# A fused Flamingo block: two PSUM banks for E slots in all stages, four for score units with 512 keys

## The reference, cut to what matters

```python
x = x + tanh(g_xattn[0]) * cross_attention(layernorm(x), ctx)      # att0: 512 keys
x = x + tanh(g_ffn[0])   * moe_top1(layernorm(x))                  # m0: 8 experts, hidden 512, ReLU
# a decoder layer on h = layernorm(x), added to x with tanh(g_xattn[1]):
h = ln(h + self_attention(h))                                      # att1: 256 keys
h = ln(h + cross_attention(h, ctx))                                # att2: 512 keys
h = ln(h + relu(h @ fc1 + b1) @ fc2 + b2)                          # f: hidden 512
# a second block on x, its output added to x with tanh(g_ffn[1]):
x = x + causal_rope_attention(rmsnorm(x))                          # att3: 256 keys
x = x + moe_top2(rmsnorm(x))                                       # m1: 4 experts, hidden 384, SiLU-gated
# each attention: softmax(q @ k.T / sqrt(8)) @ v, over all keys, head by head
```

## Time and profile before

| | before |
|---|---|
| median of 3 runs | 1185.59 us (1184.12 to 1190.38) |
| the profiled execution | 1189.5 us |
| its span, first to last instruction | 1187.5 us |
| granted TensorE clock, mean | 0.95 |
| busy: TensorE / VectorE / ScalarE / GpSimd | 1049.7 / 790.0 / 621.8 / 367.8 us |
| score matmuls, 512 keys (L1637) | 512, 403 ns each |
| maxima, 512 keys (L1304) | 512, 685 ns each |
| E matmuls (L1672) | 1408, 284 ns each |
| exponentials (L1110) | 768, 578 ns each |

### The profile page before, as it was taken

The page is one execution under the profiler, slowest core; times in us unless marked ns, Lnnn a source line. Parts: engine busy times, 40 slices in busy tenths (PEclk is TensorE's granted clock), DMA queues, the critical chain, the costliest instruction groups (busy, mean ns, idle before and its releaser), DMA issues. The chain is left out here.

```text
span 1187.5 us, 25293 instructions
## 1 busy us (share of the span) xinstructions
PE 1049.7 (88%) x8548; PEld 645.7 (54%) x8548; DVE 790.0 (67%) x1935; ACT 621.8 (52%) x1331; POOL 367.8 (31%) x982
## 2 busy tenths in 40 slices
PE   4999998799898698788799998897988889899998
PEld 1455554477454486445455554444555667656665
DVE  4788887533877524577688877869666777644443
ACT  1477764455564454456477775655644445543221
POOL 4333332221434422543433333413233435200000
PEclk9999998899987799788899999999998999999999
DMA  6655644464334663565665563543435355301000
GB/s 164 190 161 174 178 144 137 127 180 135 107 104 125 198 181 111 157 175 157 205 182 176 155 175 95 167 123 104 125 94 152 114 165 155 109 28 46 11 26 9
DMA packets 173173, 157.97 MB, mean 133 GB/s; under 512 B 13075, under 2 KB 146835, under 8 KB 172691
## 3 DMA queue, kind: packets, MB, share of 16 engines
q1 hardware_dynamic: 168854, 141.24, 40.4%
q0 software_dynamic: 4192, 15.12, 4.1%
HBM read 91.56 MB, written 66.85 MB: 133 GB/s over the span
## 5 line engine op out<-in xcount | busy, mean ns | idle before, releaser
L1110 ACT ACTIVATE prob<-ps 128x512 f32<-128x512 f32 (+1 forms) x768 | 400.2, 578 | 177.1 <-PE ps L1672 134.4
L1304 DVE TENSOR_REDUCE nmax<-ps 128x1 f32<-128x512 f32 x512 | 328.9, 685 | 82.6 <-PE ps L1637 81.3
L1672 PE MATMUL ps<-Qst,Kst 75*128 75x256 bf16 x1408 | 244.8, 284 | 15.8 <-DMA Qst<-mrow 8.7
L1637 PE MATMUL ps<-Kst,Qst 72*128 72x512 bf16 x512 | 198.7, 403 | 24.2 <-DVE nmax L1304 21.3
L1688 PE MATMUL av_ps<-prob,Vx 128*32 128x256 f32 (+1 forms) x3072 | 215.8, 398 | 0.6 <-ACT FB L1187 0.3
L1672 PEld LDWEIGHTS ps<-Qst,Kst 75*128 75x128 bf16 x1408 | 135.7, 101 | 86.5 <-ACT prob L1110 15.5
L1688 PEld LDWEIGHTS av_ps<-prob,Vx 128*32 128x32 f32 x3072 | 91.8, 114 | 66.4 <-issue 33.9
L1034 POOL TENSOR_TENSOR mparts<-nmax,zeros 128x8 bf16<-128x8 f32 x122 | 25.2, 206 | 306.1 <-issue 298.6
L1313 DVE TENSOR_REDUCE nmax<-ps 128x2 f32<-128x512 f32 x128 | 85.6, 687 | 47.9 <-PE ps L1651 47.2
L1637 PEld LDWEIGHTS ps<-Kst,Qst 72*128 72x128 bf16 x512 | 50.5, 99 | 106.6 <-DVE nmax L1304 53.2
L1114 ACT ACTIVATE OT<-av_ps 128x256 f32<-128x256 f32 x128 | 49.2, 385 | 108.7 <-PE av_ps L1688 108.1
(11 more groups left out here) (198 smaller groups left out, 1652.9 us busy)
## 6 DMA issues: line engine op xcount, KB each, us to landing
q_parts<-qp SPq DMA_DIRECT2D x96, 192.0 KB, 2.5
Qst<-q_parts SPq DMA_DIRECT2D x128, 144.0 KB
k_parts<-kp SPq DMA_DIRECT2D x46, 384.0 KB, 3.3
Kst<-k_parts SPq DMA_DIRECT2D x60, 288.0 KB
k_parts<-kp SPq DMA_DIRECT2D x48, 192.0 KB, 2.7
Kst<-k_parts SPq DMA_DIRECT2D x64, 144.0 KB
ctxT<-in_ctxT SPq DMA_DIRECT2D x16, 256.0 KB, 4.8
xs_rows<-in_blank SPq DMA_DIRECT2D x22, 128.0 KB, 4.1
```

Source lines behind the costliest of these rows:

```text
L1110: act.activation(prob[:, RING_AT[st] % RING, half * 512:half * 512 + w], bank(x)[:, 0:w], ACT.Exp).then_inc(drained(x), 1)
L1304: ve.tensor_reduce(nmax[:, g, u, h % GH:h % GH + 1], bank(st), AX.X, ALU.max, negate=True).then_inc(drained(st), 1)
L1637: last = pe.matmul(bank(st), Qst[0:ROWS, par, s, u * P:u * P + P], Ks[0:ROWS, par, s, :], start=True, stop=True)
L1672: last = pe.matmul(o, Ks[0:KROWS, par, h, t * P:t * P + P], Qst[0:KROWS, par, h, :], start=True, stop=not a.rope)
```

## The change

E steps are allowed banks 0 and 1 in every stage. Score units are allowed banks 2 to 5 with 512 keys (four in place of three), and 2 to 4 with 256 keys, as before. The smaller steps, m0.h, f.h and m1.h keep their sets, so bank 2 is now shared between score units and m0.h and f.h in stages with 512 keys too.

```diff
-    at, uses, last, low, split = {}, [0] * BANKS, list(range(-BANKS, 0)), 3, 6
+    at, uses, last, split = {}, [0] * BANKS, list(range(-BANKS, 0)), 6
     for i, st in enumerate(STEPS):
         if st[0] == "S":
-            low, split = (3, 6) if att(st[1]).keys == SC else (2, 5)
+            split = 6 if att(st[1]).keys == SC else 5
         if st[0] in E_KINDS:
-            takers, allowed = ((st, 0), (st, 1)), range(5 if st[0] == "m1.h" else low if st[0] == "E" else 3)
+            takers, allowed = ((st, 0), (st, 1)), range(5 if st[0] == "m1.h" else 2 if st[0] == "E" else 3)
         elif st[0] == "S":
-            takers, allowed = (st,), range(low, split)
+            takers, allowed = (st,), range(2, split)
```

## The result

| | before | after |
|---|---|---|
| median (range) of 5 runs | 1185.59 us (1182.02 to 1191.73) | 1209.18 us (1193.31 to 1214.32) |
| ratio to before, 95% interval | | 1.0145 [1.0097, 1.0194] |
| the profiled execution | 1189.5 us | 1209.6 us |
| its span | 1187.5 us | 1207.8 us |
| granted TensorE clock, mean | 0.95 | 0.935 |

A forecast was written before the change was run, and what follows sets the result against it. TensorE was taken to set the pace with VectorE close behind; 25.3 us of E-step costs less 20.4 us of score-unit gains made it 4.9 us slower, 1190.5 us against the 1185.6 median, range 1180 to 1201.

The forecast's parts named there:

- the direct sum: Whole kernel: 25.3 us of E-step costs minus 20.4 us of score-unit gains, so 4.9 us slower.
- the dismissal of the clock: Rival, 600 to 843 us: new pauses bring three stretches at 1.2 GHz, 10 us worse than the sum, 1200.5; chance 0.06.
- a clock below 1.00 between 600 and 843 us: Sign in the third attention stage's windows that the forecast is wrong and the clock rival holds.
- The stretch of 655 to 684 us: One batch: right if 0.5 to 1 us longer; if not, costs are covered; over 1.5 us, scores wait again.
- Cost of E's two banks: E steps on all stages wait longer for exponentials, with 1.1 us for the hidden-layer step: 25.3 us in all.
- The pair: Two E steps with only two score units between: second half's load 0.49 us later, 29 pairs, 14.2 us.
- The slots of 1.31 us: E steps with four transposes also between them: second half waits 0.19 us more in 23 slots, 4.4 us.
- Gain of the fourth score bank: Score units' 53.2 us of waits for maxima on VectorE, less those that stay: 20.4 us gained.
- "score waits" rival: Units arrive in bunches at VectorE; only 8 of the 20 us gained, 17 us slower, 1202.5; chance 0.13.
- The bank that the dense block's hidden layer shares with scores: At 771.74 us the hidden-layer step waits for a maximum to leave its bank: 1.1 us, once.
- 736 to 756 and 811 to 831 us: VectorE nearly full, score waits 9.0 and 8.6 us: 1.8 us gained each, 14.0 of 17.6 stay.
- 178 to 202 us: Behind the routing plan on VectorE, 7.1 us in five score waits: 3.8 gained, 3.3 lost.

The follow-up runs named there:

- before_look2: The kernel before, unedited, in a second further profile to see how bodies vary with nothing changed: one execution of 1201.93 us.
- e9: The changed kernel with the score units of body 16 alone back on three banks: 1.0134 against the kernel before, median 1204.99 us.
- e3: The kernel before with E steps on two banks in all stages and scores left on three: 1.0114 against the kernel before, median 1200.56 us.
- after again: The changed kernel, unedited, run once more beside the kernel before: ratio 1.0149, median 1218.98 us.
- e2: The kernel before with the change made in the third attention stage (att2) alone: 1.0068 against the kernel before, median 1196.29 us.
- e1: The kernel before with the change made in the first attention stage (att0) alone: 1.0108 against the kernel before, median 1196.73 us.
- e8: The kernel before with the dense block's activations moved from the exponentials' ring to an idle buffer: 0.9949 against before, 1194.35 us; repeated, 0.9971, 1184.57 us.
- e5: The kernel before with a fourth score bank at 512 keys, bank 6, shared with the smaller steps: 1.0983 against the kernel before, median 1318.78 us.
- e4: The kernel before with scores on four banks and E left on three, sharing bank 2: 1.0102 against the kernel before, median 1201.92 us.

## Why the prediction was wrong, point by point

**The sign was the likeliest one, the size was not.** Two steps failed. One is in the direct sum: the waits that a fourth score bank takes away were counted as time, 20.4 us of gain where the runs show 0.6, and with the cost of E's banks put too high as well the sum is some 12 us where 4.9 was forecast, as the paragraphs below work out. The other is the dismissal of the clock: "Against it: from 736 to 756 us TensorE is busy only 15.2 of 20 us, with waits for VectorE through the whole window, and the clock stays full". That row shows that waits of one kind at one place are harmless, not that new ones elsewhere will be. And the trace before has some 120 us at 1.2 GHz outside att2, so that it "does not agree for this kernel" was too much to say. I gave this rival 0.06, and in the bodies that can be compared it holds 6 of 17 us in one profile and 9 of 21 in the other: 2 to 4 us in body 4 and 3 to 5 in att2 (277.5 and 279.6 against 274.2, which is before plus the 9.2 worked out below). The forecast's own test, a clock below 1.00 between 600 and 843 us, names it. But `before_look2` has such a clock with nothing changed, so this sign alone would not have shown it. The stretch of 655 to 684 us, body 18, is 1.0 us longer, as the forecast said.

The Trainium skill's rule, "TensorE: Matmul & The Clock Gate", section "A second HAM failure mode: psum-queue depth-cycling", was cited and set aside. After, the trace agrees with it as far as the clock goes (0.51 in 606 to 613 us), and in e9 the number of banks in rotation decides how long that stretch is. That short pauses between groups of matmuls bring it about no run here shows: the pause ahead of it is one of 1.47 us, for a DMA.

**Cost of E's two banks, 25.3 us: too high by more than half.** The pair itself is right: 0.88 us from load to load becomes 1.34 to 1.35, +0.47 against 0.49. The timeline after, one such pair, which answers the earlier trace rows:

```profile
679.10 0.54 PEld L1672 LDWEIGHTS ps<-Qst,Kst 75*128 75x128 bf16 x4
679.65 0.21 PEld L1637 LDWEIGHTS ps<-Kst,Qst 72*128 72x128 bf16 x2
680.45 0.11 PEld L1672 LDWEIGHTS ps<-Qst,Kst 75*128 75x128 bf16 x2 [0.59 <-ACT prob L1110]
680.94 0.11 PEld L1672 LDWEIGHTS ps<-Qst,Kst 75*128 75x128 bf16 x2 [0.37 <-ACT prob L1110]
```

Both halves wait, as said. The slots of 1.31 us grow by 0.03, not 0.19. And what is lost in a pair is in part gained in the same body, where a score unit then finds its maximum done: the score waits of e3 fall by 8.7 us with no bank more. Together: 10.5 us in e3, where 25.3 was forecast for this half (24.2 without the bank that the hidden layer shares, which e3 doesn't share).

**Gain of the fourth score bank, 20.4 us: 0.6, and a loss of some 2 beside it.** The result is that of the "score waits" rival, only stronger, and in another form than it stated. The waits did not come back: the row fell to 15.3 us, below the 30 forecast. Their time did: TensorE stands for E, for the maxima's transposes, for a DMA or for nothing named. I subtracted from 53.2 us what VectorE or a wait just before would hold, and counted all that was left as time. A wait that goes is worth only what the next one in the same order doesn't take back.

**The direct sum, 4.9 us: about 12.** At full clock, after minus before, bodies 0 to 3 are 3.0 us longer (1.63, 0.88, 0.25, 0.24; 0.5 less in the second profile), and att2 is 9.2: body 16 by e9 +1.07, then +1.32, +0.96 and +2.57, bodies 20 and 21 together by after again +2.74, bodies 22 and 23 by e2 +0.57. 10.5 of these 12 us are E's two banks (e3), and the rest is what the fourth bank costs. Two errors of 15 and 22 us cancelled for the most part, which was luck; 7 us are left of them. Had the clock stayed as before, about 1198 us would have come out (an estimate, 1185.6 + 12.2), still within the range; the loss by the clock is what lies outside it.

**Small terms.** The bank that the dense block's hidden layer shares with scores was given 1.1 us: at slot 9 of body 21 the distance between the E steps' exponentials is 5.05 us after and 4.37 in e3, so 0.7. In the opening, 25 to 37 us, nothing was to be gained, and nothing was: its waits for maxima are 4.8 us where the earlier trace rows has 6.7, and body 0 begins at 38.16 and 37.43 us in the two profiles, 37.65 before. In 736 to 756 and 811 to 831 us, which lie in bodies 20 and 22, I allowed 1.8 us each; 1.2 each was gained by the body's end and given back within eight exponentials. In 178 to 202 us, in body 4, I took 3.8 us of gain, and the body became 2 to 4 us longer: the same stretch is granted 0.74 after, 0.86 before. TensorE is busy 12.3 of 16 us ahead of the stretch at 1.2 GHz (190 to 206.5 us, above) and without a gap in it:

```profile
178.00:202.00 24.00, 20.58 (x146) 11.46 (x146) 16.42 (x47) 10.71 (x22) 3.39 (x12) 0.74 0.45 140
174.00:190.00 16.00, 12.28 (x112) 7.18 (x113) 12.45 (x35) 8.29 (x18) 5.92 (x14) 0.99 0.49 149
```

**What stays open.** How much the fourth bank adds in whole runs: e3 and the change differ by 0.3%, and their intervals overlap, so the share of the clock above is read from profiles, two of after and one of e3. e1's runs are 1.1% slower, 13 us, but only some 2 us in bodies 0 to 3 and 2 to 3.5 in body 4 can be placed. The rest lies in bodies 5 to 15 and can't be told there from what differs between profiles of one kernel. Why body 4 falls to 1.2 GHz for as long in e2 and once in e8, and what tips bodies 20, 21 and 22, where profiles of the same kernel differ (10.2 and 3.4 us at 1.2 GHz in body 20), was not settled. Nor does time at 1.2 GHz have one price: 3.4 us of it in body 20 (after again) left nothing by the ninth exponential of body 21, and 6.8 us in body 22 left 0.1 to 0.5 by the end of body 23 (77.56 and 77.92 us, where e2 has 77.47 with none). No version with e9's cure in every body was tried.

## What to carry to other kernels

On an engine with one fixed order, the waits in a profile are not a sum of prices: take a wait away and look at the next one behind it in the same stretch before you count a gain. Size a bank rotation by what its drains need: here scores with two banks cost over 3% and with four gained nothing, a third for E was worth about 1%, and a bank shared by two drains cost more than it gave. When you compare stretches, look also at the one behind: a gain at a boundary can be gone a few us later, as here 1.2 us were. And when an edit lets TensorE run ahead, ask for what it will then stand, and check the granted clock behind that place; here, in one place, a standstill of 1.5 us went before a loss of 3.

## What the runs showed that I had not expected

- One standstill of 1.47 us, up to 604 us, is followed by 6.8 us at 1.2 GHz from 606 us on. Where the waits are spread earlier (before, e3, e9), there are 3.4 us at 1.2 GHz, which come before body 16 or reach 0.8 us into it. The body is 3.0 us longer than in e3 (31.34 against 28.35); 6.8 us at half the clock would account for 3.4.
- One bank more for scores costs 9.8% if it is the one that small steps use (e5), and 1.0% if E uses it (e4).
- Moving the dense block's activations out of the ring of exponentials makes the kernel before faster: 0.9949 and 0.9971 in two sets of runs, the second with an interval up to 1.0000. It is the only version that beat both kernels.
